# A decoder's two cross attentions: the value product with the probabilities as the stationary operand, and four key tiles loaded first

## The reference

```python
def _L1_xattn_ref(x, y, Wq, bq, Wk, bk, Wv, bv, Wo, bo):
    q = _split_heads(x @ Wq + bq)          # (8, 16, 128, 8)
    k = _split_heads(y @ Wk + bk)          # (8, 16, 77, 8)
    v = _split_heads(y @ Wv + bv)
    scores = jnp.einsum('bhqd,bhkd->bhqk', q, k) * scale
    weights = jax.nn.softmax(scores, axis=-1)
    out = jnp.einsum('bhqk,bhkd->bhqd', weights, v)
    out = out.transpose(0, 2, 1, 3).reshape(x.shape[0], x.shape[1], D_ATT)
    return out @ Wo + bo
```

## Time and profile before

| | us |
|---|---|
| median of 2 runs | 560.02 |
| the profiled execution's own time | 559.68 |
| its span, first to last instruction | 557.9 |
| TensorE matmul busy | 474.1 |
| VectorE busy | 371.1 |
| ScalarE busy | 332.8 |
| GpSimd busy | 267.3 |

### The profile page before, as it was taken

The page is one execution under the profiler, slowest core; times in us unless marked ns, Lnnn a source line. Parts: engine busy times, 40 slices in busy tenths (PEclk is TensorE's granted clock), DMA queues, the critical chain, the costliest instruction groups (busy, mean ns, idle before and its releaser), DMA issues. The chain is left out here.

```text
span 557.9 us, 9954 instructions
## 1 busy us (share of the span) xinstructions
PE 474.1 (85%) x3161; PEld 359.8 (64%) x3161; DVE 371.1 (67%) x911; ACT 332.8 (60%) x655; POOL 267.3 (48%) x294
## 2 busy tenths in 40 slices
PE   4689999999578877899994999656689779999995
PEld 3577888876356655688882578444466556777774
DVE  4787777774646745566665476767357454999995
ACT  3687777775446763356552465224467555988883
POOL 1699879777434642466662750113072231745420
PEclk9799999999779995899997899796789969999999
DMA  6614342425255000444332200003580002111101
GB/s 184 210 43 120 101 120 72 126 79 133 71 140 147 1 2 1 136 133 132 116 93 69 58 0 1 0 1 78 139 218 1 2 2 75 33 45 38 38 0 38
DMA packets 34688, 41.80 MB, mean 75 GB/s; under 512 B 5178, under 2 KB 26612, under 8 KB 34420
## 3 DMA queue, kind: packets, MB, share of 16 engines
q1 hardware_dynamic: 33796, 40.65, 26.2%
q10 hardware_dynamic: 848, 0.60, 0.4%
HBM read 30.70 MB, written 8.18 MB: 70 GB/s over the span
## 5 line engine op out<-in xcount | busy, mean ns | idle before, releaser
L1304 POOL TENSOR_TENSOR e_gc<-e_g,e_c 128x512 f32<-128x512 f32 x32 | 41.8, 1309 | 38.1 <-ACT e_g L1287 23.1
L2090 DVE TENSOR_TENSOR e_h_lo<-e_h,e_h_hi 128x512 fp32r<-128x512 f32 x56 | 55.6, 1045 | 3.4 <-ACT e_h_hi L1968 3.4
L1780 POOL TENSOR_TENSOR m_w_hi<-m_w,m_one 128x512 fp32r<-128x512 f32 x16 | 19.7, 1232 | 68.1 <-DMA m_w<-in_L_ffn_W 30.4
L963 ACT ACTIVATE x_pT<-x_turn 77x1024 f32<-77x1024 f32 x32 | 32.7, 1021 | 32.3 <-PE x_turn L901 32.3
L1964 ACT ACTIVATE e_h<-e_h,m_b 128x512 f32<-128x512 f32 x64 | 43.8, 691 | 8.3 <-PE e_h L1864 8.3
L557 ACT ACTIVATE a_p<-xn_all,a_least 128x128 f32<-128x128 f32 x128 | 40.7, 390 | 6.1 <-DVE a_least L596 6.0
L1266 ACT ACTIVATE e_h_hi<-e_h 128x512 fp32r<-128x512 f32 x34 | 21.5, 632 | 33.8 <-DVE e_h L1342 23.9
L901 PE MATMUL x_turn<-consts,x_p 128*77 128x128 f32 x256 | 38.3, 296 | 3.9 <-ACT x_p L968 3.9
L1348 DVE TENSOR_TENSOR e_h_lo<-e_h,e_h_hi 128x512 fp32r<-128x512 f32 x34 | 23.7, 698 | 26.5 <-ACT e_h_hi L1266 26.5
L703 POOL TENSOR_TENSOR a_p<-a_p,a_r 128x512 f32<-128x512 f32 x32 | 33.3, 1042 | 15.0 <-DVE a_r L605 15.0
L901 PEld LDWEIGHTS x_turn<-consts,x_p 128*77 128x77 f32 x256 | 30.3, 158 | 13.4 <-ACT x_p L968 11.1
(11 more groups left out here) (300 smaller groups left out, 1448.2 us busy)
## 6 DMA issues: line engine op xcount, KB each, us to landing
e_c<-spread SPq DMA_DIRECT2D x32, 256.0 KB, 3.3
x_ks<-kstack SPq DMA_DIRECT2D x16, 462.0 KB, 5.5
kstack<-a_blk_hi SPq DMA_DIRECT2D x32, 154.0 KB, 3.1
m_w<-in_L_ffn_W SPq DMA_DIRECT2D x16, 256.0 KB, 3.1
a_raw<-in_experts SPq DMA_DIRECT2D x17, 192.0 KB, 2.5
kstack<-a_blk_lo SPq DMA_DIRECT2D x16, 154.0 KB, 2.9
su_reversed<-scratch SPq DMA_DIRECT2D x1, 1024.0 KB, 5.6
w_wkv<-in_L_attn_Wkv SPq DMA_DIRECT2D x1, 1024.0 KB, 7.6
```

Source lines behind the costliest of these rows:

```text
L963: act.activation(pT[k % 2][:, :, :], tb[0:NKV, :, :], ACT.Copy).then_inc(S["turned_out"], 1)
L1304: pool.tensor_tensor(gc[k % 2][:, :], g[u % 2][:, :], c[k % NC][:, :], ALU.mult).then_inc(S["weighted"], 1)
L2090: dve.tensor_tensor(h_lo[half][f][:, :], h[half][f], h_hi[half][f][:, :].bitcast(F32), ALU.subtract).then_inc(S["lo_done"], 1)
```

## The change

In both layers:

- The value product has `pT` stationary (77 by 128) and `vx` moving (9 columns). The result has queries on partitions at once. It goes to `ob` for even batches and to `bk` for odd ones.
- The copy `oS` on ScalarE, the four transposes back, and the fill of `ob` with zeros go.
- VectorE's reciprocal and product (`finish`) read `ob` or `bk` directly, at lag 4 in place of 5. The slots are at lag 5 in place of 6, the projection and its addition at 6 in place of 7, the norm's statistics at 7 in place of 8.
- The last batch's `xn_all` is computed on VectorE in place of GpSimd.
- Of the logits, three batches are issued at step 18 and three at step 20, in place of five at step 18 and one at a time after.
- SyncE issues the key tiles 0 to 3 first, ahead of the copies into `qs`.

The core of the diff:

```diff
-                keys(0)
-                keys(1)
+                for b in range(KEYS):
+                    keys(b)
...
-                    if j == 0:
-                        for b in range(2, KEYS):
-                            keys(b)
...
                     if n == 2:
-                        pe.wait_ge(S["pv_zeroed"], since["pv_zeroed"] + 1)
+                        pe.wait_ge(S["q_lo_out"], since["q_lo_out"] + 2)
...
                         pe.wait_ge(S["turned_out"], since["turned_out"] + k + 1)
-                        if k % 2 == 0 and b >= 1:
-                            pe.wait_ge(S["o_out"], since["o_out"] + b)
+                        if k % 2 == 0 and b >= 2:
+                            pe.wait_ge(S["oT_out"], since["oT_out"] + b - 1)
+                        if k % 2 == 0 and b >= 4:
+                            pe.wait_ge(S["xT_out"], since["xT_out"] + b - 3)
                         for u in range(2):
-                            hg = 2 * (k % 2) + u
                             for j in range(HG):
-                                mm = pe.matmul(ob[32 * j:32 * j + VW, P * hg:P * hg + P], vx[l][:, b, HG * hg + j, :],
-                                               pT[k % 2][:, u, P * j:P * j + P], start=True, stop=True)
+                                h = HG * (2 * (k % 2) + u) + j
+                                mm = pe.matmul(acc[b % 2][:, h, 0:VW], pT[k % 2][:, u, P * j:P * j + P],
+                                               vx[l][:, b, h, :], start=True, stop=True)
                         mm.then_inc(S["pv_done"], 1)
...
-                        for hg in range(4):
-                            mm = pe.transpose(bk[:, P * hg:P * hg + P], oS[b % 2][:, P * hg:P * hg + P], ident)
-                        mm.then_inc(S["back_done"], 1)
-                    if ahead is not None and n >= STEPS + 2 and n % 2 == 0:
-                        for b in range(0 if n == STEPS + 2 else n // 2 - 5, n // 2 - 4):
+                    if ahead is not None and n > STEPS and n % 2 == 0:
+                        for b in {STEPS + 2: (0, 1, 2), STEPS + 4: (3, 4, 5), STEPS + 6: (6,), STEPS + 8: (7,)}[n]:
...
-                    b = batch_at(n, 3)
-                    if b is not None:
-                        act.wait_ge(S["pv_done"], since["pv_done"] + 2 * b + 2)
-                        if b >= 2:
-                            act.wait_ge(S["back_done"], since["back_done"] + b - 1)
-                        act.activation(oS[b % 2][:, :], ob[:, :], ACT.Copy).then_inc(S["o_out"], 1)
...
+                def finish(b):
+                    dve.wait_ge(S["pv_done"], since["pv_done"] + 2 * b + 2)
+                    dve.reciprocal(r[:, :], acc[b % 2][:, :, DH]).then_inc(S["recip_done"], 1)
+                    dve.wait_ge(S["recip_done"], since["recip_done"] + b + 1)
+                    if b >= 2:
+                        dve.wait_ge(S["slot_done"], since["slot_done"] + b - 1)
+                    dve.tensor_tensor(o[b % 2][:, :].rearrange("p (h d) -> p h d", d=DH), acc[b % 2][:, :, 0:DH],
+                                      free(r[:, 0:1], [[1, H], [0, DH]]), ALU.mult).then_inc(S["normed"], 1)
...
-                        dve.memset(ob[:, :], 0.0).then_inc(S["pv_zeroed"], 1)
...
+                    if b == B - 1:
+                        dve.wait_ge(S["rstd_done"], since["rstd_done"] + B)
+                        dve.tensor_scalar(xn_all[:, b, :], x_all[:, b, :], mv[:, b, 0:1], rstd[:, b:b + 1],
+                                          ALU.subtract, ALU.mult).then_inc(S["xn_done"], 1)
```

More of the change, by code:

```diff
@@ L738, in cross_attention @@
             m = [sb(f"m{j}", [P, 2, HG]) for j in range(2)]
-            oS = [sb(f"oS{j}", [P, 4 * P]) for j in range(2)]
             r = sb("r", [P, H])
@@ L746, in cross_attention @@
             bk = ps("back", (P, 4 * P))
-            back = bk[:, :].rearrange("p (h c) -> p h c", c=32)
+            acc = [k[:, :].rearrange("p (h c) -> p h c", c=32) for k in (ob, bk)]
             norms[0] += 1
@@ L752, in cross_attention @@
             names = ("q_done", "q_out", "scores_done", "scores_read", "max_done", "shifted", "exp_done", "turn_done",
-                     "turned_out", "pv_done", "o_out", "back_done", "recip_done", "normed", "slot_done", "oT_out",
+                     "turned_out", "pv_done", "recip_done", "normed", "slot_done", "oT_out",
                      "y_done", "with_bias", "x_out", "stats_done", "aggr_done", "var_done", "rstd_done", "xn_done",
-                     "xT_out", "pv_zeroed", "q_hi_out", "q_lo_out", "first_done", "first_hi", "first_lo") + tuple(
+                     "xT_out", "q_hi_out", "q_lo_out", "first_done", "first_hi", "first_lo") + tuple(
                          f"qs_landed{j}" for j in range(2)) + tuple(f"ks_landed{j}" for j in range(KEYS))
@@ L873, in _ @@
                             pe.wait_ge(S["normed"], since["normed"] + k + 1)
-                            mm = pe.transpose(bk[:, 0:P], o[k % 2][:, :], ident)
+                            mm = pe.transpose((ob, bk)[k % 2][:, 0:P], o[k % 2][:, :], ident)
                         else:
-                            pe.wait_ge(S["oT_out"], since["oT_out"] + B)
-                            pe.wait_ge(S["xT_out"], since["xT_out"] + k - 2)
+                            pe.wait_ge(S["oT_out"], since["oT_out"] + k - 1)
+                            pe.wait_ge(S["xT_out"], since["xT_out"] + k - 3)
                         if k >= 2:
                             pe.wait_ge(S["xn_done"], since["xn_done"] + k - 1)
-                            mm = pe.transpose(bk[:, P:2 * P], xn_all[:, k - 2, :], ident)
+                            mm = pe.transpose((ob, bk)[k % 2][:, P:2 * P], xn_all[:, k - 2, :], ident)
                         mm.then_inc(S["slot_done"], 1)
@@ L999, in _ @@
                             later_low(j)
-                        dve.wait_ge(S["q_lo_out"], since["q_lo_out"] + 2)
-                        dve.memset(ob[:, :], 0.0).then_inc(S["pv_zeroed"], 1)
                     maxima = free(m[n % 2][:, 0, 0:1], [[HG, 2], [1, HG], [0, NKV]])
@@ L1011, in _ @@
                             dve.tensor_reduce(m[n % 2][:, :, :], scores(n), AX, ALU.max).then_inc(S["max_done"], 1)
-                    b = batch_at(n, 7)
+                    if n > STEPS and batch_at(n, 4) is not None:
+                        finish(batch_at(n, 4))
+                    b = batch_at(n, 6)
                     if b is not None:
@@ L1036, in _ @@
                                           ALU.add).then_inc(S["var_done"], 1)
-                    b = batch_at(n, 5)
-                    if b is not None:
-                        dve.wait_ge(S["back_done"], since["back_done"] + b + 1)
-                        dve.reciprocal(r[:, :], back[:, :, DH]).then_inc(S["recip_done"], 1)
-                        dve.wait_ge(S["recip_done"], since["recip_done"] + b + 1)
-                        if b >= 2:
-                            dve.wait_ge(S["slot_done"], since["slot_done"] + b - 1)
-                        dve.tensor_tensor(o[b % 2][:, :].rearrange("p (h d) -> p h d", d=DH), back[:, :, 0:DH],
-                                          free(r[:, 0:1], [[1, H], [0, DH]]), ALU.mult).then_inc(S["normed"], 1)
+                    if b == B - 1:
+                        dve.wait_ge(S["rstd_done"], since["rstd_done"] + B)
+                        dve.tensor_scalar(xn_all[:, b, :], x_all[:, b, :], mv[:, b, 0:1], rstd[:, b:b + 1],
+                                          ALU.subtract, ALU.mult).then_inc(S["xn_done"], 1)
+                    if n <= STEPS and batch_at(n, 4) is not None:
+                        finish(batch_at(n, 4))
                     if ahead is not None and n == 2 * B + 4:
@@ L1069, in _ @@
                                            ALU.pow).then_inc(S["rstd_done"], 1)
+                    if b is not None and b < B - 1:
                         pool.wait_ge(S["rstd_done"], since["rstd_done"] + b + 1)
```

23 lines of the change are left out of this document (8 added, 15 removed).

## The result

The changed kernel takes 655.61 us (median of two runs, 655.07 and 656.14) against 560.02. The ratio is 1.1686, interval 1.1623 to 1.175: slower by 17%. The profiled execution's span is 653.3 us, 95.4 more than the 557.9 of before.

The account below looks back on a forecast made before the run. The prediction took the chain of turn, copy and value product as the bound. At 1.2 GHz the loops added 49.7 and 47.9 us and the drains 1.0: +98.6 on 559.7, 658 us; 8-in-10 range 574 to 665.

Parts of the forecast that it names:

- The round trip: Cross attention loops: turn, copy, value product in series set each step, 3.99 us at 2.4 GHz, 6.64 at 1.2.
- The group's price: Value product in each step: 16 records at 0.111 us, 1.78 us at 2.4 GHz, 3.55 at 1.2.
- The two first steps: First step of each layer's cross attention loop: taken as between the two clocks, 5.2 us.
- the drains: From the last turn to the copy closing the stage: +0.5 us a layer, +1.0 in total.
- the four terms: First to last turn in layers 0 and 1, +49.7 and +47.9 us; last turn to closing copy, +0.5 each.
- the sum of 98.6 us: Both cross attentions at 1.2 GHz, loops and stage ends: +98.6 us on the profiled 559.7, giving 658 us.
- The tiling rule: Value product: the skill advises against the swap; its factor of four, as an estimate, gave 1.36 us a group.
- The clock: Cross attention loops: TensorE falls to 1.2 GHz in the first steps and stays low until the mixture; chance 0.50.
- the right case: Cross attention loops: low clock throughout, 658 us, own range 645 to 668; chance 0.50.
- The rival in which the clock stays at 2.4 GHz: Cross attention loops: steps of 3.99 us, sum +16.5, 576 us; chance 0.25.
- The keys first, worth nothing: Key loads on SyncE: score products' 6.4 us of tile waits go, but inside the same 15 steps; nothing taken.
- The parts costed at nothing: Removed copy, transposes back and fill, and added waits: nothing; last `xn_all` on VectorE, with the logits' order, saves 0.8 us.

Follow-up runs that it names:

- the kernel with wide fillers: Changed kernel plus four useless products of 128 moving columns ahead of the scores of every step from 2 on: 586.94 us, ratio 1.047.
- the pair: Changed kernel plus four useless products a step, with 128 moving columns in one and nine in the other: 586.94 and 682.93 us.
- the fastest kernel of the study: Changed kernel with value product in float32r, turn ahead of the older value product, two useless 128-column products a step: 555.03 us, ratio 0.990.

## Why the prediction was right

*The round trip.* The step named as turn, copy, value product is what the trace shows, with no idle time put down to the exponentials inside it: 2.00 + 1.08 + 3.43 us against 2.02 + 1.07 + 3.55.

*The group's price.* At 2.4 GHz 0.111 us a record was forecast from the earlier trace rows, and the kernel with wide fillers gives 0.111. At 1.2 GHz I doubled it to 0.222; the changed kernel has 0.214. This is the term that was most mis-sized: with it the step is 6.51 us and not 6.64, 3.5 us less over the 28 steps. The two first steps took 4.88 and 4.61 us in place of 5.2, 0.9 less. Against these 4.5 us (by the rounded sums) stand 0.6 us that the drains took beyond their forecast and 0.8 us outside the four terms, so the sum of 98.6 us came out 3.2 over the 95.4 of span. The errors partly cancel. The range of 645 to 668 was also wider than its stated reason: a group of 3.3 to 3.7 us moves 28 steps by 7 us down and 4 up.

*The tiling rule.* The Trainium skill ("TensorEngine Tiling (Array Packing)", section "Performance Considerations") speaks against this edit, and it was right in sign. The prediction's estimate of 1.36 us put its factor of four on the wrong base, the 0.34 us that the old loads are busy. The old group took 0.61 us of the step, from 186.57 to the next turn at 187.18, and the new one takes 1.78 at the full clock: 2.9 times, within the factor of four.

*The clock.* Forecast: falls in the first steps, stays low until the mixture. Measured: 0.60 on average from 156.0 to 159.7, 0.50 from 170 to 250, every step but the first at 6.51 us. It was given half of the chance, as the prediction had only two short falls in layer 0 to argue from, one of which (159.7) came after little work and one (207.5) after much loading. They could not tell idle time from loading, and the trace has a fall in a long wait as well (395 to 400), so that the right case came first is in part luck. The reason given was nearly right: what marked the stretch before 207.5 was said to be its loads. The wide filler kernel loads as much and keeps 2.4 GHz; the pair shows that it is the few columns moved behind the loads. The rival in which the clock stays at 2.4 GHz had its steps right (3.99 us forecast, 3.99 to 4.03 measured once the clock is held). Its 576 us would still have been 11 too few for that kernel: the drains were to give 2.2 us each, and with a low clock in them they gave 0.2 and lost 1.0, and the last step of layer 1 lost another 1.6. About 3.4 us more lie outside the two cross attentions and are not explained.

*The drains.* +0.5 in layer 0, with its parts near the forecast. The last transpose of `o` starts at 258.12, 8.3 us after the last turn (8.4 forecast), and the closing copy follows 6.0 us later where it was 6.7: 0.7 saved, 0.8 forecast. In layer 1 it was +1.1, from a shorter drain before to the same 14.3 us.

*The keys first, worth nothing.* Right in the sum. No score product of the changed kernel waits for a key tile. In the kernel before the same edit is worth nothing either, for a reason the prediction didn't name: the wait moves to the fifth key tile.

*The parts costed at nothing* (the copy `oS`, the transposes back, the fill, the added waits, the last `xn_all`) were not undone one by one. The four terms leave 0.8 us of the span for whatever lies outside the two cross attentions. In the fastest kernel of the study the drains are 4.0 and 2.0 us shorter than before. Whether the removed way back gives this, or the eight records and the order of turn and value product, was not tried by itself.

## What to carry to other kernels

Where the moving operand of a product is a few columns wide, count its weight loads: each record with 128 stationary columns cost 0.111 us at 2.4 GHz and 0.215 at 1.2 here, for 9 moving columns as for 18, and what it replaces in other engines' work is worth nothing unless that work stood in the chain. Then look at the granted clock, because a TensorE full of loads with few columns moved behind them ran at 1.2 GHz, and here that cost 70 us where the longer group cost 23 net. A wait that an earlier load removed came back here at the next tile whose load did not move: look at the whole queue behind it, and at what in-order engine will be held up by what you push back.

## What the runs showed of the hardware that I had not expected

- Useless work made the kernel 69 us faster. Four products with 128 moving columns a step held 2.4 GHz; the same four with nine columns left it at 1.2 GHz and cost 27 us.
- The two levels can be so close for one program that its executions differ by 10%: 579.9 to 638.1 us.
- In float32r with the turn first, and with half of the products, layer 1 kept the full clock for its first four and six steps (2.81 and 3.10 us), while in layer 0 of the same kernels it fell within the first three. What ahead of the loop makes the difference was not tried.
